# Attention beside an expert loop: from four steps spread over 47 experts to three steps a tile, one an expert

## What is computed

```python
xn = layernorm(x)
s  = attention(xn)             # 16 query heads, one key/value head of 128; values serve as queries
g  = silu(moe(xn))             # 64 experts, 8 a token, capacity 128 here, plus a shared MLP
x  = x + s * g
xn = layernorm(x)
s  = causal_attention(xn)      # over a sequence of 2
g  = silu(ternary_mlp(xn))     # layer norm, fake quantised, GELU
x  = x + s * g
```

## Time and profile before

| what | value |
|---|---|
| median of 3 runs | 421.01 us (420.65 to 421.41) |
| the profiled execution | 421.63 us, span from first to last instruction 419.9 us |
| busy: PE, DVE, ACT, POOL | 339.9, 312.6, 213.9, 234.6 us |
| first gather, first scatter, last scatter | 52.53, 71.40, 288.94 us |
| first work on the second block's input | 296.87 us |

### The profile page before, as it was taken

How to read it: one execution, slowest core, us unless ns; L and a number is a source line. 1 busy time by engine, 2 the same in 40 slices (tenths; PEclk the granted TensorE clock), 3 DMA queues, 4 the chain that set the end, 5 groups by cost and what they waited for, 6 DMA issues and landing times.

```text
span 419.9 us, 6972 instructions
## 1 busy us (share of the span) xinstructions
PE 339.9 (81%) x2044; PEld 256.6 (61%) x2044; DVE 312.6 (74%) x989; ACT 213.9 (51%) x540; POOL 234.6 (56%) x219
## 2 busy tenths in 40 slices
PE   0999649998976788989989898884078888988893
PEld 0984425665754656767867667652057767877772
DVE  4599744667899496849786886834669988899875
ACT  3754424334545244476446444411156788777781
POOL 3610072767767368777777787845166655663311
PEclk9999957999999799999999999987559999999999
DMA  8956941776767298988787787535910000000001
GB/s 262 382 183 201 352 139 39 166 151 136 175 152 180 66 258 187 253 220 221 171 190 172 166 187 154 91 46 84 311 54 2 25 2 26 27 27 25 9 21 51
DMA packets 34041, 58.41 MB, mean 139 GB/s; under 512 B 3835, under 2 KB 20563, under 8 KB 33875
## 3 DMA queue, kind: packets, MB, share of 16 engines
q1 hardware_dynamic: 21715, 39.08, 29.6%
q0 software_dynamic: 12288, 18.88, 24.4%
HBM read 40.22 MB, written 17.73 MB: 138 GB/s over the span
## 4 chain that ended last, share of the span: by engine, by line
PE 34%; DVE 22%; issue 17%; POOL 10%; ACT 8%; DMA 8%; POOLq 0%; DVEq 0%; ACTq 0%
DMA acc_d<-W,idxE 5%; POOL acc_d L498 4%; PE two L1451 4%; PE two L1714 4%; PE two L1590 3%; PE two L1403 3%; POOL W L479 2%; PE two L1556 2%; PE two L1461 2%; DVE W L1111 2%; DVE A L996 2%; PE two L1477 2%; POOL ny L544 2%; PE two L1413 2%; PE two L1681 2%
## 5 line engine op out<-in xcount | busy, mean ns | idle before, releaser
L498 POOL DMA_INDIRECT acc_d<-W,idxE x64 | 101.7, 1590 | 52.3 <-DVE W L1111 28.1
L479 POOL DMA_INDIRECT W<-tok_d,idxE x56 | 56.8, 1015 | 46.5 <-DVE idxE L1067 29.8
L710 ACT ACTIVATE W<-two 128x256 f32<-128x256 f32 x64 | 24.4, 381 | 75.4 <-PE two L1579 70.8
L1154 DVE SCALAR_TENSOR_TENSOR W<-W,two 128x88 f32<-128x88 f32 x64 | 15.4, 241 | 47.0 <-ACT W L726 42.2
L1714 PE MATMUL two<-W,A 128*128 128x257 f16 x256 | 30.0, 273 | 10.7 <-DVE F L1333 9.9
L686 ACT ACTIVATE A<-two 128x512 f16<-128x512 f32 x32 | 19.1, 597 | 31.7 <-PE two L1535 22.8
L1714 PEld LDWEIGHTS two<-W,A 128*128 128x128 f16 x256 | 24.0, 98 | 16.3 <-DVE F L1333 11.7
L1681 PE MATMUL two<-F,wfcT 128*128 128x256 f16 x256 | 32.5, 281 | 1.5 <-DVE F L1271 1.4
L797 ACT ACTIVATE two<-two,gwv 128x512 f32<-128x512 f32 x32 | 21.4, 668 | 23.9 <-PE two L1681 23.9
L1590 PE MATMUL two<-W 128*128 128x176 f32 x160 | 32.0, 324 | 0.0
L1556 PE MATMUL two<-A,v_hi 128*128 128x256 f16 x128 | 24.5, 296 | 9.1 <-DVE A L996 9.0
(11 more groups left out here) (240 smaller groups left out, 900.2 us busy)
## 6 DMA issues: line engine op xcount, KB each, us to landing
W<-in_gu SPq DMA_DIRECT2D x20, 352.0 KB
acc_d<-F SPq DMA_DIRECT2D x2, 2176.0 KB, 14.4
F<-in_gu SPq DMA_DIRECT2D x12, 352.0 KB
W<-in_dn SPq DMA_DIRECT2D x20, 176.0 KB
tok_d<-xr SPq DMA_DIRECT2D x2, 1280.0 KB, 5.9
F<-in_dn SPq DMA_DIRECT2D x12, 176.0 KB
x<-in_q SPq DMA_DIRECT2D x4, 512.0 KB, 6.7
A<-in_Wo SPq DMA_DIRECT2D x1, 2048.0 KB, 12.4
```

Source lines behind the costliest of these rows:

```text
L479: pool.indirect_dma_start(out=xg[n % XR], out_offset=None, in_=tok_d[:, :], in_offset=bass.IndirectOffsetOnAxis(ap=idxE[:, n:n + 1], axis=0))\
L498: pool.indirect_dma_start(out=acc_d[n % 2][:, :], out_offset=bass.IndirectOffsetOnAxis(ap=idxE[:, n:n + 1], axis=0), in_=ysb[n % YS], in_o ...
L710: sc.activation(xgT[n % 2], bk_(2)[:, 0:D].rearrange("p (k n) -> p k n", k=KH), ACT.Copy)\
```

## The change

Each tile of attention now has three steps, and each expert from 15 to 62 carries exactly one: tile `t` takes experts 15+3t, 16+3t and 17+3t. Step 0 on PE is `turn_probs(t,0)` and `score(t+1)`, step 1 `turn_probs(t,1)` and the projections, step 2 `attend` for odd tiles. ACT copies `oT` at the head of step 0 and puts `exps(t+1)` ahead of `high_probs(t,1)` in step 1. DVE does `top(t+1)` in step 0 and both `take_projected` in step 2 of even tiles. The first tile's score, maximum and exponentials stand one expert earlier. The first chunk of the shared MLP's up and gate products is computed ahead of the loop, and its tanh one expert earlier. One head sum stands ahead of the loop, two at expert 0 and one at expert 17 (they were at 16, 18, 20 and 21). The last token list is built one expert earlier; for that PE also waits, before a list's matmuls, until the list before it was read. Weight sums and weight preparation move by one to three experts.

```diff
-STEPS = 4
-START, END = 15, 62
-BESIDE = NT * STEPS
+STEPS = 3
+START = 15
-SUM_AT, TERN_AT = 34, (37, 39, 42, 44, 47, 49, 52, 54)
+SUM_AT, TERN_AT = 34, (37, 38, 40, 43, 44, 46, 49, 52)
-UP_AT = {0: (0, 0), 1: (0, 1), 3: (1, 0), ...
-GATE_AT = {2: 0, 5: 1, 8: 2, 11: 3}
+UP_AT = {3: (1, 0), ...
+GATE_AT = {1: 0, 5: 1, 8: 2, 11: 3}
-HOT_AT = {..., 13: (3, 0), 14: (3, 1), 15: (3, 2)}
-NUMBER_AT = {..., 14: (3, 0), 15: (3, 1)}
-SLOTS_AT, SPREAD_AT, TURN_AT, TAKE_AT = {..., 16: 3}, {..., 17: 3}, {..., 18: 3}, {..., 19: 3}
-HEADS_AT = (16, 18, 20, 21)
-PICK_AT, DEN_AT, WEIGH_AT = 6, 19, (22, 23, 25, 27)
+HOT_AT = {..., 12: (3, 0), 13: (3, 1), 14: (3, 2)}
+NUMBER_AT = {..., 13: (3, 0), 14: (3, 1)}
+SLOTS_AT, SPREAD_AT, TURN_AT, TAKE_AT = {..., 15: 3}, {..., 16: 3}, {..., 17: 3}, {..., 18: 3}
+HEADS_AT = {0: (1, 2), 17: (3,)}
+PICK_AT, DEN_AT, WEIGH_AT = 6, 20, (22, 25, 26, 28)
-WAT, LOW_AT = 46, (47, 51, 57)
+WAT, LOW_AT = 46, (47, 50, 56)
 def beside(n):
-    done, now = [min(max(m - START, 0) * BESIDE // (END - START), BESIDE) for m in (n, n + 1)]
-    return [(k // STEPS, k % STEPS) for k in range(done, now)]
+    return [divmod(n - START, STEPS)] if START <= n < START + NT * STEPS else []
...
 ACT:  if step == 0:
+          if t % 2 == 0 and t: take_oT(t // 2 - 1)
           high_probs(t, 0)
       elif step == 1:
+          if t + 1 < NT: exps(t + 1)
           high_probs(t, 1)
 DVE:  if step == 0:
           low_probs(t, 0)
+          if t + 1 < NT: top(t + 1)
       elif step == 1:
           low_probs(t, 1)
           ...
+      elif t % 2 == 0 and t:
+          take_projected(t - 2)
+          take_projected(t - 1)
 DVE, ahead of the loop:
           select(1, NG)
+          head_sum(0)
 PE:   if step == 0:
           turn_probs(t, 0)
           if t + 1 < NT: score(t + 1)
       elif step == 1:
           turn_probs(t, 1)
           if t % 2 == 0 and t: project0(t - 2); project0(t - 1)
       elif t % 2: attend(t // 2)
 PE, ahead of the loop:
           pe.wait_ge(ld_sh, 2 * 16)
+          shared_up(0, 0)
+          shared_up(0, 1)
 PE, slots(g):
           pe.wait_ge(hot_ready, g + 1)
+          if g:
+              pe.wait_ge(idxE_ready, g)
```

More of the change, by code:

```diff
@@ L58 @@
 POS_AT = 0
-HOT_AT = {1: (1, 0), 3: (1, 1), 4: (1, 2), 7: (2, 0), 9: (2, 1), 10: (2, 2), 13: (3, 0), 14: (3, 1), 15: (3, 2)}
-NUMBER_AT = {2: (1, 0), 3: (1, 1), 8: (2, 0), 9: (2, 1), 14: (3, 0), 15: (3, 1)}
-SLOTS_AT, SPREAD_AT, TURN_AT, TAKE_AT = {5: 1, 11: 2, 16: 3}, {6: 1, 12: 2, 17: 3}, {7: 1, 13: 2, 18: 3}, {8: 1, 14: 2, 19: 3}
-HEADS_AT = (16, 18, 20, 21)
-PICK_AT, DEN_AT, WEIGH_AT = 6, 19, (22, 23, 25, 27)
+HOT_AT = {1: (1, 0), 3: (1, 1), 4: (1, 2), 7: (2, 0), 9: (2, 1), 10: (2, 2), 12: (3, 0), 13: (3, 1), 14: (3, 2)}
+NUMBER_AT = {2: (1, 0), 3: (1, 1), 8: (2, 0), 9: (2, 1), 13: (3, 0), 14: (3, 1)}
+SLOTS_AT, SPREAD_AT, TURN_AT, TAKE_AT = {5: 1, 11: 2, 15: 3}, {6: 1, 12: 2, 16: 3}, {7: 1, 13: 2, 17: 3}, {8: 1, 14: 2, 18: 3}
+HEADS_AT = {0: (1, 2), 17: (3,)}
+PICK_AT, DEN_AT, WEIGH_AT = 6, 20, (22, 25, 26, 28)
 W1_AT, W2_AT = (9, 10, 11, 12), (14, 15, 16, 17)
@@ L696, in attention_step @@
                 if step == 0:
+                    if t % 2 == 0 and t:
+                        take_oT(t // 2 - 1)
                     high_probs(t, 0)
                 elif step == 1:
-                    if t % 2 == 0 and t:
-                        take_oT(t // 2 - 1)
-                elif step == 2:
+                    if t + 1 < NT:
+                        exps(t + 1)
                     high_probs(t, 1)
-                elif t + 1 < NT:
-                    exps(t + 1)
             def turn(n):
@@ L737, in _ @@
                     shared_gate(GATE_AT[n])
-                if n == START:
+                if n == START - 1:
                     exps(0)
@@ L1001, in attention_step @@
                     low_probs(t, 0)
-                    if t % 2 and t > 1:
-                        take_projected(t - 2)
-                elif step == 1:
                     if t + 1 < NT:
                         top(t + 1)
-                elif step == 2:
+                elif step == 1:
                     low_probs(t, 1)
-                elif step == 3:
                     ve.wait_ge(probs_ready, t + 1)
@@ L1160, in _ @@
                     shared_product(PRODUCT_AT[n])
+                if n in TAKE_AT:
+                    take_indices(TAKE_AT[n])
                 if n in HOT_AT:
@@ L1170, in _ @@
                     weights_sum()
-                if n in HEADS_AT:
-                    head_sum(HEADS_AT.index(n))
+                for i in HEADS_AT.get(n, ()):
+                    head_sum(i)
                 if n in WEIGH_AT:
                     shared_weighed(4 * WEIGH_AT.index(n), 4 * WEIGH_AT.index(n) + 4)
-                if n == START - 1:
+                if n == START - 2:
                     top(0)
@@ L1541, in project0 @@
                 if t == 0:
-                    pe.wait_ge(wos_done, len(HEADS_AT))
+                    pe.wait_ge(wos_done, 4)
                 pe.matmul(bk_(1)[:, D * (1 - t % 2):D * (1 - t % 2) + D], oT[t // 2 % 2][:, P * (t % 2):P * (t % 2) + P], WoS[:, :],
```

4 lines of the change are left out of this document (1 added, 3 removed).

## The result

| what | before | after |
|---|---|---|
| median, same chip, 4 executions each | 420.86 us (420.65 to 421.41) | 406.41 us (404.95 to 408.51) |
| ratio, 95% interval | | 0.9659 [0.9613, 0.9704] |
| profiled execution: time, span | 421.63, 419.9 us | 405.89, 404.1 us |

The forecast was 408.5 us; the time came out 2.1 us lower, faster by 3.4%. The page of the changed kernel first, to be read against the earlier trace rows: PE is 9.4 us less busy although it has the same 2044 instructions, and DVE 3.7 us more.

The account below looks back on a forecast made before the run. POOL and DMA were taken to set the pace behind scatter 19, waits for put ahead of it; 9.5 us to scatter 56 plus 3.0 in the tail gave 12.5 off 421.6, 409.1, stated as 408.5; range 402.5 to 415.

Parts of the forecast that it names:

- Head: Up to scatter 0: moved chunk fills PE's idle time, DVE's head sums set the order; scatter 0 about 4.5 us earlier.
- without the head sums PE's own order would give 5.2: Bound on the gain up to scatter 0: 5.2 us if DVE's head sums were not there.
- Experts 12 to 20: Waits in DVE's queue shrink; scatter 19 at 136.6 us, 9.1 earlier, 4.6 of it won here; bounds 3 to 9.
- about 2.3 come back at expert 14: Loss at expert 14, where slots(3) waits for the fuller DVE: about 2.3 us.
- Experts 20 to 56: POOL stays the bound, attends wait 1.1 to 1.7 us each; scatter 56 at 260.6, 9.5 us earlier.
- POOL idle behind scatter 19 mostly on landings: Sign expected in the trace: behind scatter 19, POOL's idle time stands mostly on landings.
- Tail: Scatter 56 to 63: last attend moved to expert 62, landings set the pace; 15.9 us instead of 18.9, 3.0 won.
- B: Rival: each attend's wait slows PE's clock, 1.7 us more per attend, 413.5 us; chance 0.15.
- E: Rival: clock stays low through the next expert and score, 25.0 us a pair, about 432 us, slower; chance 0.05.
- C: Rival: weight loads, gathers and scatters of experts 20 to 36 crowd, landing waits double, 415 us; chance 0.10.
- D: Rival: list in experts 12 to 14 absorbed, first attend doesn't wait, 4 us more won, 404.5 us; chance 0.17.
- F: Rival: another queue carries the stalls on; time within 0.2% or a few us below; chance 0.03.

Follow-up runs that it names:

- the repeat: The changed kernel run again with no edit: median 408.65 us, ratio 0.9683 against the kernel before.
- high_probs: The changed kernel with ACT's step 1 in its old order, high_probs(t,1) ahead of exps(t+1): 410.23 us, 0.9734.
- light attend: The changed kernel without the v_lo with pT_hi product, 8 of 24 matmuls of each attend: 409.04 us, 0.9686.
- heads late: The changed kernel with the four head sums back in the loop, at experts 16, 18, 20 and 21: 412.71 us, 0.9816.
- chunk alone: The kernel before plus only shared chunk 0 moved ahead of the loop, its tanh at expert 1: 415.38 us, 0.989.
- list late: The changed kernel with the last token list one expert later, back at experts 13 to 19: 408.21 us, 0.9723.
- heads alone: The kernel before plus only the head sums moved: one ahead of the loop, two at expert 0, one at 17: 417.84 us, 0.9956.

## Why the prediction was right, step by step

**Head.** Right, in its order and in size: scatter 0 came 5.5 us earlier in the profiled execution and 5.0 in the repeat, against 4.6, and 3.5 in the two other runs with this head (high_probs, light attend), whose chunk began at the low clock. The term "two head sums to 63.5" was mis-sized by 0.8 (62.7 in the trace). The chunk's two halves took 3.60 us, which is what the sum used, and not the "1.7 us each" of the text. The bound "without the head sums PE's own order would give 5.2" held in one execution (5.0, heads late) and not in the other (7.0, chunk alone). I priced the moved chunk by its own two durations only, and left out that the matmuls behind turn(0) had run at the low clock too (0.56 in the window 52 to 65, then 1.00). With the head sums in, DVE's queue hides most of this. What the head sums cost there is 1.8 us at the full clock, and about 1 where it was low at first.

**Experts 12 to 20.** Right in the number, by another path than the forecast's. Scatter 19 was at 135.55 against 136.6 in one execution, at 139.35 in the other. The forecast let put(19), behind the first attend, release it. In the trace the attend began at 129.52, not at 131.4, the put ended at 134.4, and the scatter at 135.55 waited only the usual 0.30 behind POOL's own gather. POOL had issued without a pause since scatter 14 (119.61, and five times 3.19 us on); in the repeat it was the same from 123.42. So what set scatter 19 was scatter 14. There my term was too small: "about 2.3 come back at expert 14" came out as 3.4 (the lead of 5.46 at scatter 0 to 10 is 2.07 at scatter 14) and as 5.1 in the repeat, where the matmuls of `slots(3)` ran slow. The sign "no idle time over 2 us ahead of scatter 19" was not met either, with 2.64 us ahead of scatter 14 and 2.37 ahead of scatter 0. That two misses, an attend 1.9 us earlier and a larger loss at scatter 14, leave the sum right is luck. `slots(3)` waits for the fuller DVE as the step had it, 2.42 us, and its list was ready at 113.2 instead of 113.9. What is lost at scatter 14 goes straight to scatter 19, since POOL has no slack between them. The list's earlier place is part of it; the rest stays with the list late and came with the new steps or the small moves. That the attend's wait came from DVE's queue is shown by the heads alone (5.5 to 2.3), and that the new steps remove it too by the heads late (0.45); that the steps' pattern and the head sums must go together is shown by the heads late (0.9816). Of the parts, the head sums' gain behind the chunk was expected to be of some size alone, and is none that these runs can show (0.984 beside 0.989): they pay only with the new steps.

**Experts 20 to 56.** Right in length, 123.1 us against 124.0. PE's load doesn't bind: taking some 7 us from it changed nothing, taking the attends' waits away changed nothing, and loading the DMA queues cost 5.5 us. But the sign "POOL idle behind scatter 19 mostly on landings" was not met. Of what POOL idled beyond its 0.30 us, about 3.0 in the profiled execution stand ahead of scatters 22, 24 and 33, for a put, and 1.1 ahead of scatter 29, for a landing; in the repeat it is 2.4 and 0.9. Before, 4.4 us stood on landings and none on puts, and with the list late or the light attends landings lead again (3.8 to 1.1, 3.2 to 1.8). So the forecast's "the landings that cause them stay" holds for about the size of these waits and not for their cause. What holds those puts wasn't tried. The size of the attend's wait was too large: 1.1 to 1.7 at each in the forecast, 4.4 us in six in the trace, none over 1.04. It cost nothing either way.

**Tail.** Right: 15.6 against 15.9, and about 1.6 of the 3.3 won is the place of the last attend (17.24 with it back at expert 61). Its clock is not the rest, since the tail was 19.16 with that attend at the full clock; what is, wasn't tried by itself.

**Behind the last scatter.** Costed at nothing; the profiled execution won 1.2 us there. In the twelve other profiled executions, all with the same work there, this part lies between 129.8 and 131.5 us, so 1.2 is within what it varies by itself, and no cause in the change is shown. It is 1.2 of the 3.3 us between my 12.5 and the 15.8 of that one execution.

**The rivals.** B, an attend slowed at each wait, fell: the attends of the loop take 2.79 us behind waits of up to 1.0, and their removal gave nothing. The Trainium skill, TensorE: Matmul & The Clock Gate, Part 1, says that the throttled level is the default. I had weighed that as a price on every short wait, which the page doesn't say, and no attend of the loop in the profiled execution bears that reading out. E, which needed the same and more, fell with B; its price was also too low by its own figures (4.2 against 3.18 us over 36 experts is some 36 us, nearer 440 than 432), and its turning point is 21.0 us a pair rather than 21.5. C's mechanism is real, since doubled loads cost 5.5 us, 2.9 to 4.6 of them between scatters 19 and 30; it didn't happen, since that stretch took 38.5 us against 39.0 before. D, the list absorbed, didn't happen: 3.4 us came back at scatter 14. Yet the median, 406.4, lies as close to D's 404.5 as to the forecast's 408.5. In the profiled execution 1.2 us of that were won behind the last scatter, 0.9 at the head and 0.8 between scatters 19 and 56, and its granted clock was 0.967 against 0.954 in the repeat's. F is refuted by the 3.4%.

**What stays open.** Why one execution of the same program runs behind the 2.42 us wait at full clock and another doesn't. The medians of the changed kernel, 406.41 and 408.65 us in two sets of executions, differ by as much as the forecast missed by, so a sum of a few terms can't be tested closer than about 2 us here, and the 0.2% that I gave as what a measurement can tell was too small: the ratios' intervals are 0.5% and more to either side. What the tail gained beyond the place of one attend is open as well, and so is what holds the puts behind scatter 19. The step pattern wasn't run with both the old list and the old head sums.

## What to carry to other kernels

Put work into an idle stretch of PE even where nothing waits for it: beside its own time it can win back the clock of what follows, though how much differs from execution to execution (7.0 and 5.0 us here). When a scatter comes on time, look also at what released it: here the number was right and its path wasn't. When a queue's moved work is set against a stall it relieves, price it at both places; here the head sums cost at the head all that they gave until the steps changed too. And before freeing one engine, ask which stage it bounds: some 7 us less for PE, and the waits ahead of its attends, were worth nothing behind an issuing POOL, while eight doubled weight loads cost 5.5 us.

## What the hardware showed that I had not expected

**A wait doesn't decide the clock.** The same wait of 2.42 us ahead of the same 16 matmuls (2.41 once) stood in eight executions. In four they took 1.92 us, in the others 2.71, 2.89, 3.12 and 3.33 us. The 1.41 us ahead of the last attend were followed by the low level (0.61 us for two matmuls, 1.2 GHz) before the change and by the high one (0.39, 2.4 GHz) in the run with the attend at expert 61. The changed kernel's eight times run from 404.95 to 411.09. How much of that is the clock isn't shown: its two profiled executions had 0.967 and 404.1 us, 0.954 and 409.3 us, but one of 409.77 us had a mean granted clock of 0.968.

**POOL's additions block DVE's.** Three DVE additions of 128x128 f32 took 4.50, 2.44 and 1.31 us beside POOL's additions, and 0.28 to 0.29 without. The Trainium skill, SBUF — State Buffer, section "SBUF: two separate sides", says that VectorE and GpSimd share a pair of ports by an exclusive lock: whichever of a VectorE operation with two SBUF inputs and a GpSimd operation that reads SBUF starts first holds it for the whole instruction, and the other waits. The trace agrees closely. By columns, POOL's 8.72 us for 2048 + 1024 + 512 are by estimate 5.0, 2.5 and 1.2, so that its additions end at about 27.5, 30.0 and 31.2, and the last at 32.0 (31.31 + 0.73). DVE's long ones end at 27.46, 30.03, 31.38 and 32.12: each was held to the end of one POOL addition, and a single one, 0.28 at 27.39, came through between two.
